# The first FFN written out and joined to the second attention's block; first expert tiles ahead of the last sums

## What is computed

```python
x = x + tanh(g_xattn[0]) * xattn0(layernorm(x), ctx)          # 16 heads of 8
x = x + tanh(g_ffn[0]) * ffn0(layernorm(x))                   # below
x = x + tanh(g_xattn[1]) * xattn1(layernorm(x), ctx)          # 16 heads of 64
x = x + tanh(g_ffn[1]) * ffn1(layernorm(x))                   # 8 experts, argmax routing

# ffn0: layernorm once more, then
x_attn = xn @ attn_w.T + attn_b + flat
h   = gelu(x_attn of expert block e @ w1[e] + b1[e])          # blocks by position, not by routing
eo  = h @ w2[e] + b2[e]
out = gelu(eo @ next_w.T + next_b)
# ffn1: per token, e = argmax(router logits); down_w[e] @ (silu(gate_w[e] @ x) * (up_w[e] @ x))
```

## Time and profile before

| | |
|---|---|
| median of 3 runs | 789.6 us (787.2 to 789.66) |
| the profiled execution, its own time | 788.38 us |
| its span | 786.6 us |
| mean granted TensorE clock | 0.979 |
| busy: TensorE, VectorE, ScalarE, GpSimd | 751.0, 620.0, 547.7, 463.3 us |
| first FFN, by TensorE's work | 205.4 to 285.8 us on the span's clock |
| second attention and second FFN | from 287.9 us |

### The profile page before, as it was taken

How to read it: one execution, slowest core, us unless ns; L and a number is a source line. 1 busy time by engine, 2 the same in 40 slices (tenths; PEclk the granted TensorE clock), 3 DMA queues, 4 the chain that set the end, 5 groups by cost and what they waited for, 6 DMA issues and landing times.

```text
span 786.6 us, 30077 instructions
## 1 busy us (share of the span) xinstructions
PE 751.0 (95%) x10516; PEld 626.3 (80%) x10516; DVE 620.0 (79%) x2413; ACT 547.7 (70%) x1105; POOL 463.3 (59%) x867
## 2 busy tenths in 40 slices
PE   5899999999999989999999999999999999989994
PEld 2688888887788867888888888888888888768884
DVE  5699999998777767788888888887899888775552
ACT  2588888886555567777777777777776777656762
POOL 5445777873022246676767677676776667436553
PEclk8599999999999999999999999999999999999997
DMA  8903999900200000000000000000000100003200
GB/s 250 295 3 109 281 271 233 227 4 3 75 1 0 0 1 2 2 9 7 0 7 7 7 3 3 7 7 7 1 6 7 36 20 0 8 16 94 69 31 13
DMA packets 56323, 41.72 MB, mean 53 GB/s; under 512 B 3929, under 2 KB 51811, under 8 KB 56016
## 3 DMA queue, kind: packets, MB, share of 16 engines
q1 hardware_dynamic: 52848, 36.53, 17.7%
q0 software_dynamic: 2272, 4.27, 1.7%
q10 hardware_dynamic: 1152, 0.27, 0.2%
HBM read 18.07 MB, written 23.44 MB: 53 GB/s over the span
## 4 chain that ended last, share of the span: by engine, by line
PE 56%; DVE 4%; issue 1%; ACT 1%; POOL 1%; DVEq 0%; ACTq 0%; POOLq 0%
PE l_pv L2050 15%; PE l_qk_bank L56 12%; PE l_tz L56 10%; PE l_b L2016 5%; PE l_pv L1189 3%; PE l_b L2011 3%; PE l_a L56 2%; PE l_a L1994 2%; PE l_b L1180 1%; PE l_b L56 1%; DVE l_neg_max L1379 1%; PE l_pv L2027 1%; DVE x_sb L1402 1%; PE l_tz L1159 1%; PE l_a L2001 0%
## 5 line engine op out<-in xcount | busy, mean ns | idle before, releaser
L2050 PE MATMUL l_pv<-l_Z,l_probs 128*128 128x129 f32 x1024 | 163.8, 284 | 2.2 <-ACT l_probs L1865 1.4
L2050 PEld LDWEIGHTS l_pv<-l_Z,l_probs 128*128 128x128 f32 x1024 | 138.5, 191 | 21.4 <-DVE l_acc L1402 4.6
L1794 POOL TENSOR_TENSOR l_qk_lo<-w,l_qk_hi 128x512 f16<-128x512 f32 x128 | 144.5, 1160 | 0.6 <-ACT l_qk_hi L1859 0.6
L1402 DVE SCALAR_TENSOR_TENSOR x_sb<-l_pv,l_inv,x_sb 128x128 f32 (+1 forms) x256 | 89.8, 351 | 30.9 <-DVE l_inv L1389 6.0
L1865 ACT ACTIVATE l_probs<-l_b 128x512 f32<-128x512 f32 x128 | 72.7, 594 | 52.6 <-PE l_b L2016 52.5
L56 PE MATMUL l_tz<-M,cT 128*128 128x512 f16 x384 | 104.1, 380 | 1.6 <-DVE l_T_lo L1373 1.1
L1855 ACT ACTIVATE w<-l_qk_bank 128x512 f32<-128x512 f32 x124 | 74.1, 597 | 41.9 <-PE l_qk_bank L56 40.1
L505 DVE TENSOR_REDUCE n_shared<-fold_bank 128x4 f32<-128x512 f32 x128 | 87.1, 680 | 12.7 <-PE fold_bank L742 10.3
L1379 DVE TENSOR_REDUCE l_neg_max<-l_a 128x4 f32<-128x512 f32 x128 | 83.2, 681 | 3.5 <-PE l_a L1994 3.2
L1859 ACT ACTIVATE l_qk_hi<-w 128x512 f16<-128x512 f32 x124 | 77.4, 624 | 1.1
L1870 ACT ACTIVATE l_Z<-l_tz 128x512 f32<-128x512 f32 x124 | 74.3, 599 | 5.4 <-PE l_tz L56 1.8
(11 more groups left out here) (321 smaller groups left out, 2269.3 us busy)
## 6 DMA issues: line engine op xcount, KB each, us to landing
expert_rows<-empty_row SPq DMA_DIRECT2D x8, 2178.0 KB, 23.9
x_sb<-expert_rows SPq DMA_DIRECT2D x39, 66.0 KB, 1.8
w<-in_L_ffn_w SPq DMA_DIRECT2D x1, 2048.0 KB, 9.4
x_sb<-in_x SPq DMA_DIRECT2D x3, 512.0 KB, 7.5
ctx_sb<-in_ctx SPq DMA_DIRECT2D x3, 512.0 KB, 8.5
w_raw<-in_L_ffn_gate_w SPq DMA_DIRECT2D x1, 1408.0 KB, 10.3
w_raw<-in_L_ffn_up_w SPq DMA_DIRECT2D x1, 1408.0 KB, 12.5
downT<-in_L_ffn_down_w SPq DMA_DIRECT2D x2, 512.0 KB, 4.0
```

What stands on the lines that cost most here:

```text
L1402: nc.vector.scalar_tensor_tensor(out=total, in0=O[:, h, 0:P], scalar=inv[:, j:j + 1], in1=total, op0=ALU.mult, op1=ALU.add).then_inc(summe ...
L1794: nc.gpsimd.tensor_tensor(qk_lo[:, w, m, Q * u:Q * u + Q].rearrange("p t n -> p (t n)"), qk[:, u, m, :], qk_hi[:, w, m, Q * u:Q * u + Q].r ...
L2050: last = nc.tensor.matmul(pv_bank[m % 2][:, h * (P + 1):(h + 1) * (P + 1)], probs[:, 2 * m + h, :], Z[:, w, 2 * m + h, :], start=True, sto ...
```

## The change

`first_ffn` becomes a class, `FirstFfn`, with one method for each of the pieces above. Its block is gone: `second_attention` makes the object and calls its methods in its own block, for pairs 0 to 15 without a loop. Work for pairs beyond 15 is left out. VectorE's clearing of constants and the statistics of sequences 0 and 1 move into pairs 10 to 13 (`prime`); four projection steps, two transposes and the first context products stand between the products of pairs 14 and 15, without `keep_awake`. ScalarE's copies of the projections stand there too, and the load of Exp's table comes after them. The second attention's eight banks are the first FFN's, and the tiles `hid`, `znT` and `xaT` lie in `probs` and `rowsT`; the normalised rows lie in the spare rows of x_sb. GpSimd does `deviations` for pairs 4 to 15, before it waits for the priming. The way back of pair 15 waits for the sums to x of pair 14. At the end, the transposes of tiles 3 to 5 move to just behind the last scores by key; VectorE does the gatings (`hidden`) of tiles 0 and 1 ahead of the last two sums; and the routing's calls stand later among the tiles' calls.

The diff, cut to its core (the bodies of the methods are those of the block before):

```diff
-    k.norms.xn = k.w_raw[:, 0:8 * P].rearrange("p (w s u n) -> p w s u n", w=2, s=2, u=2)
+    k.norms.xn = k.x_sb[:, B:B + AHEAD, 0:P].rearrange("p (w s u) n -> p w s u n", w=2, s=2)
...
+    def vector_begin(self, dve):
+        nc, k = self.nc, self.k
+        nc.vector.memset(self.unit[:, 0:1], 0.0).then_inc(self.primed, 1)
+        nc.vector.memset(self.unit[:, 2:3], 0.0).then_inc(self.x_done, 2)
+        dve.wait_ge(k.ffn0_landed, k.ffn0_total)
+        k.folded_lo(dve, 2)
+        self.transposed(dve, 0)
+        k.folded_lo(dve, 3)
+        self.attended(dve, 0)
+        self.transposed(dve, 1)
+        self.norms.normalised(dve, 2, 0)
+
+    def vector_step(self, dve, g):
+        if g + 1 < PAIRS:
+            self.attended(dve, g + 1)
+        if g + 2 < PAIRS:
+            self.transposed(dve, g + 2)
+        if g + 3 < PAIRS:
+            self.norms.normalised(dve, g + 3, (g + 3) % 2)
+        if g + 4 < PAIRS:
+            self.norms.statistics(dve, g + 4, g % 2)
+        if g + 1 < PAIRS:
+            self.add_to_x(dve, g)
...
+    def way_back(self, pe, g):
+        if g + 1 == PAIRS:
+            pe.wait_ge(self.x_done, 2 * PAIRS)
+        pe.wait_ge(self.outT_ready, g + 1)
...
-        tz_bank, qk_bank = (ctx.enter_context(nc.psum_tensor(f"l1_{name}", [P, 512], F32)) for name in ("tz", "qk_bank"))
...
+        qk_bank, tz_bank = f0.t_bank, f0.hid_bank[0]
+        b_bank = f0.hid_bank[1:3]
+        a_bank = (f0.hid_bank[3], f0.eo_bank)
+        pv_bank = (f0.next_bank, f0.attn_bank)
...
-        first_qk = (qk_bank, b_bank[1], qk_bank, b_bank[1])
+        first_qk = (qk_bank, qk_bank, qk_bank, b_bank[1])
...
+                def prime(g):
+                    if g == 10:
...
+                        statistics(0, 0)
+                        statistics(1, 1)
+                    elif g == 11:
+                        nc.vector.memset(neg_max[:, :], 0.0).then_inc(primed, 1)
+                        nc.vector.memset(Z[:, :, :, P:P + 1], 1.0).then_inc(primed, 1)
+                        nc.vector.tensor_scalar(bias_row[:, :], k.bo[:, 1, :], k.tg[:, 1:2], None, ALU.mult).then_inc(primed, 1)
...
+                    elif g == 12:
+                        nc.vector.memset(qk[:, 0, 0, 0:1], 0.0).then_inc(qk_lo_ready, 4)
+                        nc.vector.memset(acc[:, :, :], 0.0).then_inc(x_done, 2)
...
+                    elif g == 13:
+                        for e in range(E):
+                            nc.vector.memset(less8[:, e:e + 1], float(e - E)).then_inc(consts, 1)
+                            nc.vector.memset(region[:, e:e + 1], float(e * REGION)).then_inc(consts, 1)
+                            nc.vector.memset(ends[:, e:e + 1], float(e * REGION)).then_inc(consts, 1)
...
+                f0.vector_begin(dve)
+                for g in range(PAIRS):
+                    f0.vector_step(dve, g)
+                    prime(g)
+                transposed_lo(0, first_T[0])
                 first_z_out(0)
-                transposed_lo(0, first_T[0])
+                f0.add_to_x(dve, PAIRS - 1)
...
-                for m in range(6, 8):
-                    sums(B - 1, 1, m)
-
                 j = PAIRS - 1
                 ffn.hidden(dve, 0, 0)
+                sums(B - 1, 1, 6)
+                ffn.hidden(dve, 0, 1)
+                sums(B - 1, 1, 7)
                 ffn.transposed_lo(dve, 1)
-                ffn.hidden(dve, 0, 1)
+                ffn.hidden(dve, 0, 2)
+                ffn.results(dve, 0, 0)
                 for v in range(2):
                     rows_transposed(j, v)
                 rows_summed(j)
-                ffn.hidden(dve, 0, 2)
+                ffn.hidden(dve, 1, 0)
                 dve.wait_ge(row_summed, 2 * j + 2)
                 rows_aggregated(j)
                 rows_variances(j)
-                ffn.results(dve, 0, 0)
+                ffn.results(dve, 0, 1)
...
-                ffn.hidden(dve, 1, 0)
-                ffn.results(dve, 0, 1)
+                ffn.hidden(dve, 1, 1)
+                ffn.transposed_lo(dve, 2)
+                ffn.results(dve, 0, 2)
                 ranks_out(j)
                 for part in range(4):
                     put(j, part)
-                ffn.hidden(dve, 1, 1)
...
+                f0.scalar_begin(act)
+                for g in range(PAIRS - 1):
+                    f0.second_out(act, g)
+                    f0.next_out(act, g)
+                    if g == PAIRS - 2:
+                        first_projected(0)
+                    f0.hidden(act, g + 1)
+                first_projected(1)
+                f0.second_out(act, PAIRS - 1)
+                act.wait_ge(T_moved, 2)
+                transposed_hi(0, first_T[0])
+                f0.next_out(act, PAIRS - 1)
+                first_projected(2)
+                first_projected(3)
+                act.wait_ge(primed, 1)
+
+                nc.scalar.activation(carrier[:, 2:3], carrier[:, 0:1], ACT.Exp).then_inc(exp_done, 4)
                 transposed_hi(1, first_T[1])
...
                 ffn.gated(act, 0, 0)
+                ffn.transposed_hi(act, 1)
                 ffn.gated(act, 0, 1)
-                ffn.transposed_hi(act, 1)
...
-                awake(2)
-                project(0, 1, 0, first=0)
+                f0.tensor_begin(pe)
+                for g in range(PAIRS - 1):
+                    f0.second_product(pe, g)
+                    f0.attend(pe, g + 1)
+                    if g + 2 < PAIRS:
+                        f0.transpose(pe, g + 2)
+                    f0.next_product(pe, g)
+                    if g == PAIRS - 2:
+                        project(0, 1, 0, first=0)
+                    f0.first_product(pe, g + 1)
+                    f0.way_back(pe, g)
+                project(0, 1, 1, first=1)
+                f0.second_product(pe, PAIRS - 1)
+                for n in range(2):
+                    transpose(n, n, first_T[n])
                 project_context(0, 0, 0, first=True)
...
+                f0.next_product(pe, PAIRS - 1)
+                project(0, 0, 0, first=2)
+                f0.way_back(pe, PAIRS - 1)
+                project(0, 0, 1, first=0, bank=b_bank[1])
                 project_context(0, 0, 1, first=True)
-                awake(1)
                 score_by_query(0, 0, 0, wait=False)
                 project_context(0, 0, 2, first=True)
-                awake(2)
                 score_by_query(0, 0, 1, wait=False)
...
                     score_by_key(n, u, 1)
+                    if not left:
+                        ffn.transpose(pe, 1)
...
                 for m in range(6, 8):
                     weigh(B - 1, 1, m)
-                ffn.transpose(pe, 1)
                 ffn.transpose_hidden(pe, 0)
                 ffn.first_products(pe, 0, 2)
                 ffn.transpose_hidden(pe, 1)
                 pe.wait_ge(summed, 16 * B + 2)
                 ffn.second_product(pe, 0)
+                ffn.first_products(pe, 1, 0)
                 for v in range(2):
                     route_transpose(PAIRS - 1, v)
-                ffn.first_products(pe, 1, 0)
-                route_logits(PAIRS - 1)
                 ffn.transpose_hidden(pe, 2)
                 ffn.transpose(pe, 2)
                 ffn.second_product(pe, 1)
                 ffn.first_products(pe, 1, 1)
-                route_ranks(PAIRS - 1)
+                route_logits(PAIRS - 1)
                 ffn.transpose_hidden(pe, 3)
                 ffn.second_product(pe, 2)
                 ffn.first_products(pe, 1, 2)
+                route_ranks(PAIRS - 1)
```

293 lines of the change are left out of this document (118 added, 175 removed).

## The result

The changed kernel took **781.1 us** (median of 4 runs, 778.5 to 782.5), the kernel before 789.6 (4 runs): ratio 0.9891, 95% interval [0.986, 0.9923], so 8.5 us faster, with 6.1 to 11.1 by the interval. Its profiled execution took 778.47 (span 776.7), the shortest of the four. Predicted were 780.8, in a range from 778 to 785.

A forecast was written before the change was run, and what follows sets the result against it. TensorE, busy 95% of the span, was taken to bound the kernel. Gains of 5.8 and 3.0 summed to 8.8 us, off the median of 789.6: 780.8 us, range 778 to 782.3, or to 785 with Rival (a).

The forecast's parts named there:

- Part 1: Last pairs of the first FFN and second attention's opening: removed work, boundary and interleaving gain 5.8 us, bounds 4.0 to 6.5.
- were the load hidden: Second attention's opening: upper bound of 6.5 us gain if Exp's table load were off the path.
- rival (b): First FFN's end: Copy needs its own table, so copies between gelus cost four loads, 5.1 us; 785.9 us; chance 0.04.
- Rival (c): First FFN's 16 pairs: written-out code starves the engines, 0.7 us per pair; 2.4 us slower, 792.0 us; chance 0.08.
- the price of priming: VectorE's memsets and statistics in pairs 10 to 13: costed at 0, without cover 0.1 up to 3 us.
- Part 2: Tail, last sums and second FFN's first tiles: reordering gains 3.0 us, bounds 1.2 to 4.4.
- the wait of 1.29: Tail, ahead of tile 3's second product: its result now precedes ranks and lists, so 3.3 us is gained by there.
- Two new waits of 0.3 and 0.1, for results behind list parts: Tail, after tile 3's second product up to tile 9: small new TensorE waits that lower the gain to 3.0 us.
- The late rows: Tail: their first three loads land by 713.0, normalisation is due at 713.7; covered by 0.7 us, so no limit.
- is not edited; what comes to it earlier leaves it as much earlier: Second attention's steady loop: passes on the time gained before it in full, with no loss.
- Rival (a): Opening or tail: late ScalarE handoffs, late rows or lists leave gains of 5 to 7.2, 782.4 to 784.8 us; chance 0.2.
- Rival (d): Opening and tail: reorderings do nothing, tail under 0.5 us, removed work alone 3.5 us; 786.1 us; chance 0.04.

The follow-up runs named there:

- the second profile: The changed kernel measured again without an edit; ratio 0.9895 to the kernel before.
- group 1: Runs timed together: changed kernel again, it with the old tail, and the kernel before with only the new tail or only the first FFN written out; kernel before 796.0 us.
- more_tables: Changed kernel with two more table loads (Exp, then Gelu) and their small activations ahead of the load of Exp's table; ratio 0.9955 to the kernel before.
- group 2: Four edits of the changed kernel timed together: opening behind last pair, list operations two by two, T_hi before Exp's load, two more loads; kernel before 796.5 us.
- group 3: Timed together: changed kernel with list operations late and T_hi first (0.9863), changed kernel with late rows loaded later (0.9994), kernel before profiled again (788.3 us).

## Why the prediction was right, and where it was not

- **Part 1**, 5.8: measured 5.64, and 5.65 in the second profile. The steps held, too: second product of the last pair 6.33 us behind pair 14's (6.23 by my sum), maxima 10.22 behind it (10.15), T_lo's end 8.36 behind it (8.30). ScalarE's steps, which I had just ahead of their users, made none wait by 0.15 or more. The bound "were the load hidden" was 0.65 better; the run that hid it gave 0.52. One Gelu and one Exp were loaded: rival (b) is out.
- **The written-out pairs**: 5.02 from pair to pair, with the memsets in pairs 10 to 13 too. Rival (c) and the price of priming are out.
- **Part 2**, 3.0: measured 2.53. The first step fell as worked out: the gating starts at 686.32, 1.95 behind the start of the table load, where it stood 3.54 behind it. Tile 3's second product, the wait of 1.29, gained 3.05 (3.3 by my sum), with a wait of 0.21 left ahead of it (695.93). The term that was mis-sized is "Two new waits of 0.3 and 0.1, for results behind list parts": from there to tile 7's second product the gain falls by 0.5, to 2.52, in steps of 0.2 and 0.1 a tile without a wait over 0.1 on TensorE. In that stretch VectorE, with the list parts between its gatings and results, has almost no idle time (0.19 us from 697.54 to 702.23); which of its operations hold the tiles up I haven't followed. The late rows were no limit, as I had it (0.7 in hand by my sum, 1.1 measured).
- **What failed** is the sentence that the second attention's loop "is not edited; what comes to it earlier leaves it as much earlier". It leaves it 1.52 us later relative to its start, since VectorE's list operations met GpSimd's subtractions at another phase. Rival (a) had a loss of that size, but in other places: neither ScalarE's handoffs nor the late rows held the changed kernel up. Its 784.8 is a gain of 4.8, not the 5 beside it (784.6). Rival (d) is out with 5.64 and 2.53.
- The traces' sum is therefore 5.64 + 2.53 + 0.05 - 1.52 = 6.7; the medians say 8.5 with an interval from 6.1. The clock's fall at the old boundary, in one of the four profiles that have it whole, is one thing that a single pair of profiles leaves out. The number was met closely, and in part by luck: what single profiles leave out went against a loss of 1.5.
- In group 1 the gain has the same ratio, and another make-up: nothing lost in the six steps against the two kernels with the old opening, and less than 2.5 won in the tail up to tile 12.

## What to carry to other kernels

Surplus work in a loop's last turns is often a filler: taking it out gives back only what the waits under it leave (1.69 of 2.76 us here), and the rest comes when the next stage's first work is put there (2.80). A stage that isn't edited still changes when another engine's phase against it moves, so compare it step by step before calling it untouched. Where VectorE does small operations from memory to memory beside GpSimd's long ones, place them in GpSimd's idle time: here that was worth 1.8 us to one kernel and 3.4 to the other, beside 2.5 for the whole reordering of the tail.

## What the runs showed of the hardware

- A VectorE operation on 8 numbers that takes 0.15 us alone lasts up to 1.09 us if it starts under a GpSimd tensor_tensor, one on 128x16 up to 1.20, and it ends with GpSimd's. ScalarE showed nothing of the kind (597 ns for 128x512 beside GpSimd's subtractions as without). VectorE operations that read PSUM and one tensor in memory (351 ns beside GpSimd as without) did not wait. This is what the Trainium skill (SBUF — State Buffer, "Who interferes with whom") says of the port pair that the two share, and that it is held for a whole instruction; by the traces it holds for the 1x8 shift, cast and scaling too.
- At the block's boundary TensorE idle for 2.07 us kept a granted clock of 1.00; idle for 2.45 there, or for 3.23 in `more_tables`, it was granted 0.50 next, and 1.00 again 3 to 5 us after it had resumed. Yet the length of the idle time doesn't settle it: at the boundary before the first FFN, near 200 us, it is 1.3 to 1.5 us in all 14 profiles, and the clock of 196 to 206 us is 0.83 in eight of them and 1.00 in six. The slower work behind such a wait comes on top of it: 3.0 us of waiting cost 4.7 in all.
- In the first 40 us the granted clock differed from run to run (0.59 to 0.83 in 10 to 20 us, 0.50 to 0.66 in 20 to 30, 0.60 to 1.00 in 30 to 40) and pair 14 came at 272.5 to 276.7: as much as executions of one kernel differ (778.5 to 782.5).
- In groups 1 and 2 TensorE stood for 3 to 5 us in the tail, VectorE and ScalarE with it, and the profile names no data for it. The changed kernel has it in group 1 and not in its first profile, and one chip shows it in all four kernels of group 2 and in none of group 3.
